# Two-layer graph kernel on one Trainium2 core: clearings moved to SyncE's queue, and another order inside the front and inside a related tile

## What is computed

```
h = relu(layernorm(x))
q = h[sub] @ Wq.T + bq ; k = h[obj] @ Wk.T + bk           # 8 heads of 64, pairs (sub, obj) below 1500
scores[:, sub, obj] = (q * k).sum(-1) / 8, other adjacent pairs 0, the diagonal 1e-7, not adjacent -inf
x = x + (softmax(scores).sum(heads) / 8) @ h              # first layer
h = relu(layernorm(x)) ; seq = h @ W_seq
second layer: 16 heads, leaky_relu(score1[i] + score2[j]), masked softmax over all 2048, @ seq, @ W_out, elu
x = x + that
```

## Time and profile before

| | before |
|---|---|
| median of three runs | 1186.28 us |
| the profiled execution's own time | 1189.33 us |
| its span | 1187.4 us |
| busy share of the span: PE / DVE / ACT / POOL | 93% / 80% / 68% / 10% |
| mean granted clock of PE | 0.981 |
| chain that ended last: PE / DMA / issue / POOL / ACT / DVE | 75% / 7% / 5% / 5% / 5% / 2% |

### The profile page before, as it was taken

One profiled execution on the slowest core, in us unless ns is written; L12 is line 12 of the kernel. 1 busy time (PEld: TensorE's weight loads), 2 busy tenths in 40 slices (PEclk: granted clock), 3 DMA queues, 4 the chain that ended last, 5 costly groups with the idle time before them and its releaser, 6 DMA issues.

```text
span 1187.4 us, 24638 instructions
## 1 busy us (share of the span) xinstructions
PE 1102.9 (93%) x10565; PEld 764.9 (64%) x10565; DVE 952.3 (80%) x1325; ACT 806.8 (68%) x843; POOL 122.2 (10%) x141
## 2 busy tenths in 40 slices
PE   4999969999999999999897899999999999999997
PEld 3444424444444444444343899999999999999843
DVE  3543517988998999998853899999999999999565
ACT  1343326766667766666624999998999999999122
POOL 2678640000000000000000000000000000000011
PEclk9999987999999999999999999999999999999999
DMA  9531544122222121100342111011001111111311
GB/s 343 130 28 16 129 79 100 34 43 64 65 65 54 38 49 46 36 36 27 125 168 101 64 38 38 38 38 38 38 38 38 38 38 38 38 38 38 108 71 71
DMA packets 37245, 77.69 MB, mean 65 GB/s; under 512 B 5653, under 2 KB 13714, under 8 KB 35090
## 3 DMA queue, kind: packets, MB, share of 16 engines
q1 hardware_dynamic: 30402, 65.26, 15.7%
q0 software_dynamic: 6736, 10.86, 6.4%
HBM read 65.39 MB, written 23.21 MB: 75 GB/s over the span
## 4 chain that ended last, share of the span: by engine, by line
PE 75%; DMA 7%; issue 5%; POOL 5%; ACT 5%; DVE 2%; SPq 0%; DVEq 0%; POOLq 0%; ACTq 0%
PE psum L1573 14%; PE psum L737 12%; PE psum L652 11%; PE psum L1570 8%; PE psum L1571 8%; PE psum L1574 8%; DMA rel_planes<-f_ones,f_flat 5%; PE psum L756 5%; PE psum L1668 5%; POOL rel_planes L156 5%; PE psum L707 2%; ACT area_b L947 2%; ACT area_h L1417 2%; DMA rel_planes<-f_h 1%; PE psum L727 1%
## 5 line engine op out<-in xcount | busy, mean ns | idle before, releaser
L1417 ACT ACTIVATE area_h<-area_a,keep 128x2048 fp8e4<-128x2048 f32 x208 | 397.1, 1993 | 1.2 <-DMA area_a<-s_rows 1.2
L1573 PE MATMUL psum<-s_V,area_h 128*128 128x198 bf16 x2048 | 285.5, 248 | 0.0
L1574 PE MATMUL psum<-s_V,late 128*128 128x99 bf16 x2048 | 279.5, 208 | 0.0
L1570 PE MATMUL psum<-s_V,area_h 128*128 128x99 bf16 x2048 | 206.0, 210 | 11.4 <-DVE area_b L1472 10.7
L1571 PE MATMUL psum<-s_V,area_b 128*128 128x99 bf16 x2048 | 205.9, 209 | 0.0
L1573 PEld LDWEIGHTS psum<-s_V,area_h 128*128 128x128 fp8e4 x2048 | 199.4, 97 | 0.1
L1574 PEld LDWEIGHTS psum<-s_V,late 128*128 128x128 fp8e4 x2048 | 199.3, 97 | 0.0
L1570 PEld LDWEIGHTS psum<-s_V,area_h 128*128 128x128 fp8e4 x2048 | 189.5, 98 | 12.8 <-issue 10.9
L1571 PEld LDWEIGHTS psum<-s_V,area_b 128*128 128x128 fp8e4 x2048 | 189.6, 98 | 0.0
L737 PE MATMUL psum<-area_h,f_region 128*128 128x512 f32 x384 | 181.6, 598 | 0.0
L1156 DVE CUSTOM_DVE_ANT_0 area_b<-psum,late 128x1500 f32<-128x1500 f32 x96 | 161.4, 1717 | 24.0 <-PE psum L652 21.6
(11 more groups left out here) (172 smaller groups left out, 1178.0 us busy)
## 6 DMA issues: line engine op xcount, KB each, us to landing
area_a<-s_rows SPq DMA_DIRECT2D x16, 1024.0 KB, 4.8
late<-rel_planes SPq DMA_DIRECT2D x36, 192.0 KB, 2.7
rel_planes<-f_h SPq DMA_DIRECT2D x2, 2304.0 KB, 22.8
area_h<-in_x SPq DMA_DIRECT2D x4, 1024.0 KB, 12.4
keep<-in_adj POOLq DMA_DIRECT2D x16, 256.0 KB, 5.9
f_region<-in_x SPq DMA_DIRECT2D x16, 256.0 KB, 2.7
x<-f_region SPq DMA_DIRECT2D x16, 256.0 KB, 2.0
area_a<-adj_chunks SPq DMA_DIRECT2D x4, 1024.0 KB, 9.0
```

The costliest lines, as they stand in the source:

```text
L1417: act.activation(masks[:, j, :], s1b[:, b, :], ACT.Relu, bias=t["s2"][:, n, 0, j:j + 1], scale=BIG, saturate=False).then_inc(signs, 1)
L1570: pe.matmul(out[:, :, 0:DZ], masks[:, j, cols], V[:, b, j, :, 0:DZ], **first)
L1573: pe.matmul(out, masks[:, j, cols], V[:, b, j, :, :], **first)
L1574: last = pe.matmul(out[:, :, DZ:CZ], nadjT[:, NEAR_TILES.index(j), cols], V[:, b, j, :, DZ:CZ], **then)
```

## The change

In the front all three planes are cleared from SP's queue, in the order plane 0, `load_x(0)`, plane 1, `load_w(K)`, plane 2, `load_w(Q)`, and SP waits only for the first of the two memsets. POOL no longer issues a clearing. `PLANE` gives plane 0 two columns in a row at the start where it gave three. `LATE_LOADS` are after 60 and 74 scatters. On PE the second gather turns tiles 2 and 3, the third turns only tile 5, and tile 6 is turned after it, between the scores, which are now computed as pairs with `score(0, 1)` to `score(0, 3)` where there was `score_head`. ACT's front follows.

In a step PE keeps the same work in another order. Piece 0's second block is summed after `turn_one_and_scores`. `turn_h` comes before the last sum where it came after it. The second, third and fourth pair of scores come after two, four and six of the eight pieces' sums where they came after three, five and seven, and the third and fourth adjacency quarter come earlier. ACT's `make_low` and `relu` go to the start of the step, `copy_h` and `edges` come before the last `exp`, and `edges` gets a wait for all masks. The rounds' list in `bank_rounds` and `PLACE`, `ORDER` follow. The diff, cut to its core:

```diff
...
 NU = NT - ET
-PLANE = (0,) * 3 + tuple((i + 1) % PLANES for i in range(EC - 3))
-LATE_LOADS = {56: ADJ_RING, 72: ADJ_RING + 1}
+PLANE = (0,) + tuple(i % PLANES for i in range(EC - 1))
+LATE_LOADS = {60: ADJ_RING, 74: ADJ_RING + 1}
 def tile_at(k):
...
         def load_w(i, name):
...
         sp.dma_start(rel[0:EP, :, :], io["L0_gnn_rel_pair_index"].rearrange("(p c) s -> p c s", p=EP)).then_inc(rel_in, 16)
+        sp.wait_ge(zero_set, 1)
+        f.clear_plane(sp, t, 0)
         load_x(0)
+        f.clear_plane(sp, t, 1)
         load_w(K, "L0_gnn_Wk")
-        sp.wait_ge(zero_set, 2)
-        for i in range(1, PLANES):
-            f.clear_plane(sp, t, i)
+        f.clear_plane(sp, t, 2)
         load_w(Q, "L0_gnn_Wq")
...
         pool.wait_ge(zero_set, 2)
-        f.clear_plane(pool, t, 0)
         pool.memset(t["ident"][:, :], 0.0).then_inc(s["zeroed"], 1)
...
     def turns(n, *ms):
         return [("w", n - 1, m) for m in ms if 1 <= n <= ET]
-    order = adj(1, NU) + adj(2) + adj(NU + 1) + [("h", 0)] + adj(3, NU + 2) + [("proj", 0), ("one", -1), ("h", 1)]
+    order = adj(1, NU) + adj(2, 3) + [("h", 0)] + adj(NU + 1) + [("proj", 0), ("one", -1), ("h", 1)] + adj(NU + 2)
     for n in range(ET - 1):
...
         order += turns(n, 0) + [("proj", n + 1), ("one", n)] + turns(n, 2) + [quarter[0]] + turns(n, 3, 4) + [quarter[1]]
-        order += turns(n, 5, 6) + [quarter[2]] + turns(n, 7) + [quarter[3], ("h", n + 2)]
+        order += turns(n, 5) + [quarter[2]] + turns(n, 6) + [quarter[3]] + turns(n, 7) + [("h", n + 2)]
     order += turns(ET - 1, 0) + [("proj", ET), ("one", ET - 1)] + turns(ET - 1, 2, 3, 4, 5, 6) + [("h", ET + 1)]
...
     PAIRS = HA // 2
-    PLACE = {0: 0, 1: 1, 2: 0, 3: 1, NU: 2, NU + 1: 2, NU + 2: 2}
-    ORDER = (0, 1, NU, 2, NU + 1, 3) + tuple(range(NU + 2, NT))
+    PLACE = {0: 0, 1: 1, 2: 0, 3: 2, NU: 2, NU + 1: 1, NU + 2: 2}
+    ORDER = (0, 1, NU, 2, 3) + tuple(range(NU + 1, NT))
     GROUPS = 6 * KT
...
             store_chunk(2)
-            store_chunk(NU + 1)
             load_x(3)
+            store_chunk(3)
             store_x(1)
...
             load_related(1)
-            store_chunk(3)
-            store_chunk(NU + 2)
+            store_chunk(NU + 1)
             store_x(2)
...
             load_related(2)
+            store_seq(0)
+            store_chunk(NU + 2)
             load_related(3)
-            store_seq(0)
             for n in range(NT - 2):
...
                     gather(1, i)
-                    turn_adj(2 if i < 4 else NU + 1, i % 4)
+                    turn_adj(3 if i % 2 else 2, i // 2)
                 turn_h(0)
...
                     gather(2, i)
-                    turn_adj(NU + 2 if i % 2 else 3, i // 2)
+                    if i % 2:
+                        turn_adj(NU + 1, i // 2)
                 project(0)
+                score(0, 1)
                 turn_one_and_scores(-1)
                 turn_h(1)
-                for hd in range(2, HA):
-                    score_head(0, hd)
+                turn_adj(NU + 2, 0)
+                score(0, 2)
+                turn_adj(NU + 2, 1)
+                score(0, 3)
+                for q in (2, 3):
+                    turn_adj(NU + 2, q)
             def step(n):
...
                 project(n + 1)
-                add_blocks(n, 0)
+                add_blocks(n, 0, (0,))
                 turn_one_and_scores(n)
+                add_blocks(n, 0, (1,))
                 if turned:
...
                     turn_adj(ka, 0)
-                add_blocks(n, 2)
+                if scored:
+                    score(n + 1, 1)
                 if turned:
                     turn_w(r, 3)
-                if scored:
-                    score(n + 1, 1)
+                add_blocks(n, 2)
                 if turned:
...
                     turn_adj(ka, 1)
-                add_blocks(n, 4)
+                if scored:
+                    score(n + 1, 2)
                 if turned:
                     turn_w(r, 5)
-                if scored:
-                    score(n + 1, 2)
+                add_blocks(n, 4, (0,))
+                if chunked:
+                    turn_adj(ka, 2)
+                add_blocks(n, 4, (1,))
                 if turned:
...
                 if chunked:
-                    turn_adj(ka, 2)
-                add_blocks(n, 6)
+                    turn_adj(ka, 3)
+                if scored:
+                    score(n + 1, 3)
                 if turned:
                     turn_w(r, 7)
-                if scored:
-                    score(n + 1, 3)
-                if chunked:
-                    turn_adj(ka, 3)
+                add_blocks(n, 6)
+                turn_h(n + 2)
                 add_blocks(n, 7)
-                turn_h(n + 2)
             def last_steps():
...
             def edges(r):
                 b = r % 2
+                act.wait_ge(masked, HA * (r + 1))
                 act.activation(e0[:, b, :], negm[:, b, :], ACT.Exp).then_inc(efac, 1)
...
                     copy_adj(2, q)
+                    copy_adj(3, q)
                 for i in range(PLANES):
...
                 relu(0)
+                copy_h(0)
                 for q in range(4):
                     copy_adj(NU + 1, q)
-                copy_h(0)
-                for q in range(4):
-                    copy_adj(3, q)
-                    copy_adj(NU + 2, q)
+                relu(1)
+                exp(0, 0)
                 projected(0)
+                exp(0, 1)
                 copy_one_and_scores(-1)
-                relu(1)
                 copy_h(1)
-                for hd in range(2):
-                    exp(0, hd)
                 count(0)
-                for hd in range(2, HA):
-                    exp(0, hd)
-                    if hd == 5:
-                        f.make_low(act, 1)
+                exp(0, 2)
+                copy_adj(NU + 2, 0)
+                exp(0, 3)
+                copy_adj(NU + 2, 1)
+                exp(0, 4)
+                exp(0, 5)
+                copy_adj(NU + 2, 2)
+                f.make_low(act, 1)
+                copy_adj(NU + 2, 3)
+                exp(0, 6)
+                exp(0, 7)
                 edges(0)
             def step(n):
...
                     copy_w(r, 0).then_inc(evicted, 1)
-                if n < ET:
-                    start_w(n)
+                start_w(n)
+                if n + 2 < ET:
+                    f.make_low(act, n + 2)
+                relu(n + 2)
                 projected(n + 1)
...
                     copy_w(r, 2).then_inc(evicted, 1)
+                if scored:
+                    exp(n + 1, 0)
                 if chunked:
...
                 if scored:
-                    exp(n + 1, 0)
+                    exp(n + 1, 1)
                 if turned:
...
                 if scored:
-                    exp(n + 1, 1)
                     count(n + 1)
...
                     copy_w(r, 4).then_inc(evicted, 1)
+                if scored:
+                    exp(n + 1, 2)
                 if chunked:
...
                 if scored:
-                    exp(n + 1, 2)
+                    exp(n + 1, 3)
                 if turned:
                     copy_w(r, 5).then_inc(evicted, 1)
-                if scored:
-                    exp(n + 1, 3)
-                if n + 2 < ET:
-                    f.make_low(act, n + 2)
+                if chunked:
+                    copy_adj(ka, 2)
                 if turned:
                     copy_w(r, 6).then_inc(evicted, 1)
-                if chunked:
-                    copy_adj(ka, 2)
                 if scored:
                     exp(n + 1, 4)
-                if turned:
-                    copy_w(r, 7).then_inc(evicted, 1)
-                if n + 2 < NT:
-                    relu(n + 2)
-                if scored:
-                    exp(n + 1, 5)
                 if chunked:
...
                 if scored:
+                    exp(n + 1, 5)
+                if turned:
+                    copy_w(r, 7).then_inc(evicted, 1)
+                if scored:
                     exp(n + 1, 6)
-                if n + 2 < NT:
-                    copy_h(n + 2)
+                copy_h(n + 2)
                 if scored:
+                    edges(n + 1)
                     exp(n + 1, 7)
-                    edges(n + 1)
             def last_steps():
...
```

17 lines of the change are left out of this document (9 added, 8 removed).

## The result

The changed kernel takes **1170.63 us** in the median of four runs (1168.47 to 1173.64), the kernel before 1186.26 (1185.34 to 1186.77): a ratio of 0.987, 95% interval 0.9853 to 0.9887. That is 15.6 us less. The forecast was 1170.3 us, in a range from 1163 to 1179. The runs spread over 5.2 us where those of before spread over 1.4. The profiled execution took 1171.58 us, 1.0 above its median.

The account below looks back on a forecast made before the run. Waits lengthened PE's and DVE's step loops (33.2 and 33.3 us without them); scatters bounded the front. Steps -19.2 and front +3.2 made -16.0: profiled 1189.33 became 1173.3, less 3.05 above the median, 1170.3 us; range 1163 to 1179.

Parts of the forecast that it names:

- The steps, -19.2: All eleven related-tile steps: summed gain of 19.2 us, with the steady step going from 35.2 to 33.5 us.
- Item (1): Step's seam: turning h before the last sum removes PE's 1.43 us idleness; next step begins 0.65 us after the last mask.
- Item (2): PE's step: half of piece 0's sum (0.9 us) after the score columns covers a 0.59 us idleness.
- Item (3): Step's second pair of scores comes 2.1 us earlier, more than DVE's 1.39 us wait; third and fourth pairs likewise.
- Item (4): ACT's step: `make_low` and `relu`, 2.5 us together, precede the copy of the projection; cost at most 0.1 us.
- Item (5): ACT's step end: `edges` before the last exponential is the same work in another order, nothing gained.
- Item (6): DVE's `finish` needs the last sum, ending about 1.2 us after the last mask; 0.7 us idleness absorbs it, no effect.
- The front, +3.2: Front: the first related tile's last mask ends at 201.4 us, a cost of 3.2 us.
- Gain of the scatters 2.5 us: Front: earlier clearing brings the tenth scatter from 43.03 to 40.6 us, and that gain of 2.5 us lasts.
- The steady loop at 34.5: Rival: DVE and PE wait for each other, steps stay at 34.5 us, kernel 1181.0 us; chance 0.13.
- One queue at 183 GB/s: Rival: SP's queue alone is limited to 183 GB/s, front some 23 us later, kernel 1190.1 us; chance 0.04.
- Half clock throughout the front: Rival: all first-tile score pairs and the first step's scores run at half clock, +7 us, kernel 1174.1 us; chance 0.22.

Follow-up runs that it names:

- front alone: The kernel before with only the change's front (clearings, scatters, order of chunks, paired scores, queue) and its old steps: 1190.65 us, ratio 1.0035.
- steps alone: The kernel before with only the change's step order on PE and ACT, edge factors' place and rounds, and its old front: 1164.69 us, ratio 0.9832.
- heads one by one: The changed kernel with heads 2 to 7 of the first related tile scored singly instead of in pairs: 1177.59 us.
- Heads with other planes: The changed kernel with heads 2 to 7 scored singly and columns 1 to 4 sent to planes 0, 1, 0, 1 before plane 2: 1168.04 us.
- piece 0 in one: The changed kernel with both blocks of piece 0 summed ahead of the second layer's score columns again: 1171.79 us.
- h last: The changed kernel with the turn of the next tile's h behind the last sum again: 1178.44 us.
- second pair late: The changed kernel with the second pair of scores back where it stood, one turn and one sum later, ACT's order kept: 1191.72 us.
- old clearings: The changed kernel with the clearings, their order among the loads and the planes' first columns as before: 1175.08 us.
- load out: Tile 6's load moved after the planes' read-back: in the changed kernel 1166.64 us; also with heads scored singly and the planes' first columns reordered 1168.83 us.

## Why the prediction was right, and where it was wrong

**The steps, -19.2: right, a little too small.** The trace gives -19.9, the medians -20.0 (changed kernel less front alone) and -21.3 (steps alone less before). By terms, forecast and measured: seven steady steps 11.9 and 12.5, steps 9 and 10 2.2 and 2.3, step 0 1.9 and 1.7, step 1 3.2 and 3.5. The steady step is 33.43 against 33.5 forecast; the bound of 33.3 from DVE's row was the true one. "PE and DVE are then tied" failed: with the half sum undone PE's wait of 0.59 came back and the step did not move. DVE holds the step alone.

**Item (1), the turn of h.** The idleness at the seam went as forecast, and PE begins the next step 0.76 us after the last mask, for 0.65. PE's wait of 1.43 us was not its worth: undone under the new ACT order it costs 0.96, through DVE's factors.

**Item (2), half of piece 0's sum,** covers 0.59 us of PE as forecast, and is worth nothing, since PE isn't the bound.

**Item (3), the second pair,** was priced by the wait in the earlier trace rows, 1.39 us. Undone it costs 1.97, of which 0.77 are PE's wait for a copy that only ACT's new order puts late. The price of 1.39 was right, with the 0.23 before each later pair that went too; what undoing one half of a change costs is not what that half had gained.

**Item (4)**, 0.1 us on the copy of the projection: 0.16. **Item (5)**, the edge factors reorder nothing: true while the copy of h is in time; behind a late copy they are the path. **Item (6)**, `finish`: no wait in the steady steps.

**The front, +3.2: the sign right, both terms wrong.** "Gain of the scatters 2.5 us" failed: their beginning was nearly as forecast (the first at 12.1 for 11, the fourth at 28.9 for 29.2, the tenth at 39.8 for 40.6; PE's first transposition at 22.7 for 22.3), but "after that both kernels are the same" is false. The eightieth scatter starts no earlier; the later stretch took it back. The first mask at 173.68 seemed to confirm 173.1, and only since the profile of before had a late one. The pairs: "28.3 us from first mask to last" was 25.2 (25.5 with the front alone), since the pairs took 4.48, 2.79 and 4.29 us for 5.8, 5.6 and 2.8, and DVE had less to wait. The price at half clock was misread as well: the 6.23 us at 178.88 are two heads one after the other, the clock 0.50 for most of them, and not a pair; six matmuls of one head at 0.50 take 5.37, and a head alone takes as long as a pair. Against the 22.65 of the earlier trace rows that is +2.6; against the 20.6 with the steps alone it is +4.6. So 3.2 was 4.7 to 5.9, because the scatters gave nothing, the reference was a slow execution, and the 0.85 us in step 0 were not thought of.

**The sum, -16.0 against -15.6,** is thus 0.7 to 2.1 us too little gain in the steps and 1.5 to 2.7 us too little loss in the front: that 1170.3 holds to 0.3 us is luck, since the errors cancel.

**The rivals.** The steady loop at 34.5: no, 33.43. One queue at 183 GB/s: no, plane 0 was cleared by 12 us and plane 2 by 29. Half clock throughout the front: not in the changed kernel's profile (0.89 in the mean), but one run here, heads one by one, shows it at 0.67 with a first tile of 33.0 us. The Trainium skill (TensorE: Matmul & The Clock Gate, HAM oscillation) describes bursts that each start at the half clock behind the waits between them. Read as "every pair is slow", as in the prediction, this trace doesn't bear it out: of the changed kernel's four pairs behind waits of 3.84, 0.39, 2.73 and 2.04 us, between 177 and 202 us, the first and the third were slow. Heads with other planes, whose waits between 170 and 200 us were at most 1.02 us, kept a clock of 1.00 there.

## What to carry to other kernels

Take the bound from the loop of each engine, not from the idleness of the busiest: here PE was busy for 94% of a step, and the 1.8 us came from waits in DVE's loop, whose length without them gave the new step to 0.1 us. A part that is undone alone, with its partner left changed, shows the price of that mixture. Compare a stretch that differs by 5 us from execution to execution by kernels that hold one half of the change, not by two profiles. An earlier start in a queue of 80 transfers is worth nothing until its end is seen to move; taking one load out from between them went with 4.0 us less in one kernel and with nothing in another.

## What the runs showed of the hardware

The granted clock from 170 to 200 us was 0.67 in one execution and 1.00 in another of the same PE program. Six runs of heads one by one spread over 11.4 us, fifteen of the kernel before over 7.1. A fall doesn't follow idleness by any rule that these runs show: one pair of scores took 4.27 us behind 7.1 us of unbroken work and 2.22 of idleness; another, in the kernel with piece 0 in one, took 2.79 behind 3.13 of idleness. Ahead of the very first pair, at some 152 us, PE idled for 2.11 us in every kernel with the new order of chunks; the pair took 4.48 us in the changed kernel, the front alone and the kernel with h last, and 2.79 in those with the second pair late, with the old clearings and with piece 0 in one. What decides it stays open.

One head's six score matmuls, on 64 rows, took 2.78 us at a granted clock of 1.00 (heads with other planes, 179.82), and a pair's twelve, issued in turn on the two halves of the rows, 2.79 (changed kernel, 185.04). One head took 5.37 us at 0.50 (heads one by one, 190.78).

Scatters waited 2.4 to 3.4 us for an earlier one to land where a 256 KB adjacency load had been issued a few places ahead in their queue, and 1.9 to 2.3 us in four places where none had (148.53 with the steps alone, 122.54 with the old clearings, 158.11 and 158.06 in the two kernels with the load out). With one such load taken out, the stretch from the 74th scatter to the 80th took 10.5 and 11.4 us, of which the issue of the load had been 0.9; with it they took 10.9 to 14.7. How much of the rest is the load's, these runs don't show.
